# A decoder layer on one core: when GpSimd may subtract in the early tiles, and an output projection in four steps

## The reference, cut to what matters

```
x = x + self_attention(layernorm(x))           # 16 heads of 16, 4 key/value heads, projection @ Wo + bo
x = x + cross_attention(layernorm(x), context) # 77 context rows
x = x + ffn(layernorm(x))                      # shared expert + the 2 best of 8 experts, by a softmax gate
```

## Time and profile before

| | |
|---|---|
| median of 3 runs | 1723.9 us (1721.14 to 1726.04) |
| the profiled execution | 1722.33 us, its span 1720.6 us, mean granted clock 0.980 |
| PE busy | 1665.3 us (97%) |
| DVE busy | 1386.6 us (81%) |
| ACT busy | 1097.4 us (64%) |
| POOL busy | 399.6 us (23%) |
| output projection | 744.6 to 805.5 us |
| early tiles with routing | 1185.8 to 1244.1 us |

### The profile page before, as it was taken

The page is one execution under the profiler, slowest core; times in us unless marked ns, Lnnn a source line. Parts: engine busy times, 40 slices in busy tenths (PEclk is TensorE's granted clock), DMA queues, the critical chain, the costliest instruction groups (busy, mean ns, idle before and its releaser), DMA issues. The chain is left out here.

```text
span 1720.6 us, 35427 instructions
## 1 busy us (share of the span) xinstructions
PE 1665.3 (97%) x11830; PEld 1092.0 (63%) x11831; DVE 1386.6 (81%) x2603; ACT 1097.4 (64%) x2272; POOL 399.6 (23%) x462
## 2 busy tenths in 40 slices
PE   7899999999999999999999999997899999999998
PEld 3443333333333333366689999996798888888887
DVE  6699999999999999634688999985897666666664
ACT  5348888888888888842577777774325455554552
POOL 2000000000000000041042222222472554555540
PEclk9869999999999999999999999998999999999999
DMA  6612111111111111153311321114525333333335
GB/s 217 196 20 36 33 32 30 31 30 30 30 31 30 30 31 31 37 169 109 120 49 43 105 99 52 41 56 155 188 78 169 55 49 54 52 52 55 49 58 169
DMA packets 93594, 124.80 MB, mean 73 GB/s; under 512 B 19307, under 2 KB 72863, under 8 KB 92863
## 3 DMA queue, kind: packets, MB, share of 16 engines
q1 hardware_dynamic: 75696, 99.34, 20.4%
q0 software_dynamic: 13728, 18.88, 6.8%
q10 hardware_dynamic: 4047, 4.91, 0.9%
HBM read 71.25 MB, written 46.60 MB: 68 GB/s over the span
## 5 line engine op out<-in xcount | busy, mean ns | idle before, releaser
L506 DVE TENSOR_REDUCE half_max<-psA 128x1 f32<-128x512 f32 x1024 | 630.1, 683 | 6.7 <-PE psA L559 4.6
L538 ACT ACTIVATE PT<-psB 128x1024 f32<-128x1024 f32 x512 | 520.8, 1026 | 140.1 <-PE psB L569 139.7
L559 PE MATMUL psA<-KS,QS 48*128 48x512 f32 x1024 | 397.5, 470 | 8.0 <-PEq L104 2.0
L569 PE MATMUL psB<-QS,KS 50*128 50x512 f32 x1024 | 377.8, 457 | 0.1
L588 PE MATMUL psO<-PT,VG 128*32 128x256 f32 x4096 | 321.0, 392 | 0.1
L559 PEld LDWEIGHTS psA<-KS,QS 48*128 48x128 f32 x1024 | 163.3, 191 | 232.8 <-DVE half_max L506 172.9
L588 PEld LDWEIGHTS psO<-PT,VG 128*32 128x32 f32 x4096 | 84.6, 108 | 176.2 <-issue 102.8
L1405 ACT ACTIVATE x_probs<-x_scores,x_neg_max 128x77 f32<-128x77 f32 x512 | 176.3, 359 | 6.4 <-DVE x_neg_max L1308 6.3
L1880 PE MATMUL m_psY<-swd_high,m_hT 128*128 128x256 f32 x760 | 157.8, 291 | 0.4 <-DVE m_hT L2034 0.2
L569 PEld LDWEIGHTS psB<-QS,KS 50*128 50x128 f32 x1024 | 150.9, 186 | 10.7 <-ACT PT L538 9.5
L475 POOL CAST max_parts<-neg_max 128x16 fp32r<-128x16 f32 x32 | 6.3, 197 | 618.4 <-DVE neg_max L516 618.4
(11 more groups left out here) (235 smaller groups left out, 2727.2 us busy)
## 6 DMA issues: line engine op xcount, KB each, us to landing
QS<-q_parts SPq DMA_DIRECT2D x96, 128.0 KB
q_parts<-part SPq DMA_DIRECT2D x16, 512.0 KB, 4.3
OT<-OU SPq DMA_DIRECT2D x16, 512.0 KB, 3.5
mx_kept<-cx_mx SPq DMA_DIRECT2D x8, 616.0 KB, 5.4
cx_mx<-mx_kept SPq DMA_DIRECT2D x4, 1232.0 KB, 7.7
KS<-k_parts SPq DMA_DIRECT2D x32, 128.0 KB
xf_rows<-XF SPq DMA_DIRECT2D x32, 128.0 KB, 1.7
acc<-X SPq DMA_DIRECT2D x32, 128.0 KB, 1.8
```

The lines of the kernel that those rows point to most:

```text
L506: dve.tensor_reduce(half_max[:, h * (TB // 2) + t % (TB // 2), n:n + 1], psA[:, bank_of(slot, 2 * v + r), :], axis=AX.X, op=ALU.max).then_ ...
L538: act.activation(PT[:, k % 4, 2 * a:2 * a + 2, :].rearrange("p h n -> p (h n)"), psB[:, u % 2, :, :].rearrange("p a n -> p (a n)"), ACT.Ex ...
L559: pe.matmul(psA[:, bank_of(slot, m), :], QS[top:top + KQ, slot, h // 2, t * P:(t + 1) * P], KS[top:top + KQ, slot, n * HALF:(n + 1) * HALF ...
L569: mm = pe.matmul(psB[:, u % 2, r, :], KS[top:top + KM, slot, c * P:(c + 1) * P], QS[top:top + KM, slot, a, half * HALF:(half + 1) * HALF], ...
```

## The change

Two independent edits.

In the output projection the copies to OT are gone: psR's transposes read OU itself. TensorE's step n now runs psR of tile n, psU of tile n-2 and psY of tile n-3, and VectorE's addition to X moves to the same step as psY. VectorE's loop is written out.

In the early tiles VectorE raises a new semaphore `pieces_done` after each first and each second piece. Up to step 8 GpSimd waits for the first piece of step s before it subtracts tile s, and for the second before it subtracts a weight part. Weight parts are halves (128x512), one in each of the steps 1 to 8, which makes two experts instead of three; the third expert's matrices join those of VectorE (12 instead of 10, up to step 24). ScalarE's casts for the first experts begin at step 1 instead of 2, and SP no longer waits in step 3.

```
-POOL_EXPERTS = 3
+POOL_EXPERTS = 2
-POOL_FROM = 2
+POOL_FROM = 1
+POOL_HALVES = KD * POOL_SPLITS
...
             for s in range(EARLY_TILES):
+                if s < HOT_AT:
+                    pool.wait_ge(pieces_done, 2 * s + 1)
                 if low_on_pool(s):
                     token_low(s)
-                for k in splits_at(s):
-                    if k < POOL_SPLITS:
-                        weight_part_low(k)
+                if 0 <= s - POOL_FROM < POOL_HALVES:
+                    pool.wait_ge(pieces_done, 2 * s + 2)
+                    weight_half_low(s - POOL_FROM)
...
+            def weight_half_low(n):
+                k, half = divmod(n, KD)
                 x, m = SPLITS[k]
                 w, high, low = SPLIT[m]
                 pool.wait_ge(w_high, k + 1)
+                pool.tensor_tensor(low[:, x, half, :], w[:, x, half, :], high[:, x, half, :], ALU.subtract).then_inc(lows_pool, 1)
...
                 if beside:
                     first_piece(now[0])
+                    dve.sem_inc(pieces_done, 1)
...
                 if beside:
                     second_piece(now[0])
+                    dve.sem_inc(pieces_done, 1)
```

The projection, TensorE's part (VectorE's addition moves from `tile(2)` to `tile(L_OUT)`; all of `load_rows` and its waits go):

```
+        L_TURN, L_OUT = 2, 3
...
             def step(tile):
+                if t := tile(0):
+                    i, e = t
+                    if not peeled(i, 2):
+                        pe.wait_ge(norm_done, at(i, 1, -1))
+                    for g in range(NKV):
+                        mm = pe.transpose(psR[:, e, g * P:(g + 1) * P], OU[:, g, i * P:(i + 1) * P], ident[:, :])
+                    mm.then_inc(rows_done, 1)
+                if t := tile(L_TURN):
...
+                if t := tile(L_OUT):
...
-            for n in range(NT + 2):
+            for n in range(NT + L_OUT):
```

More of the change, by code:

```diff
@@ L647, in self_out_places @@
     offset = T["place"]["QS"] + 4608
-    for name, shape in (("wo_sb", [P, KD, D]), ("bo_sb", [P, D]), ("OT", [P, 2, NKV, 2 * P])):
+    for name, shape in (("wo_sb", [P, KD, D]), ("bo_sb", [P, D])):
         T[name] = nc.alloc_sbuf_tensor_at(name, shape, F32, offset=offset)
@@ L651, in self_out_places @@
     assert offset <= T["place"]["QS"] + 4 * 2 * (GH // 2) * S
-def load_rows(eng, T, n):
-    eng.dma_start(T["OT"][:, n % 2, :, :], T["OU"][:, :, 2 * n * P:(2 * n + 2) * P]).then_inc(T["so_sums_in"][n % 2], 16)
 def load_self_out(eng, T):
@@ L661, in load_self_out @@
     eng.dma_start(T["bo_sb"][:, :], T["bo"].rearrange("(a n) -> a n", a=1).to_broadcast([P, D])).then_inc(T["so_w_in"], 16)
-    for n in range(2):
-        load_rows(eng, T, n)
 def phase_self_out(nc, T):
@@ L674, in sem @@
             return ctx.enter_context(nc.semaphore(name))
-        wo, bo, OT, w_in, sums_in = (T[k] for k in ("wo_sb", "bo_sb", "OT", "so_w_in", "so_sums_in"))
+        wo, bo, OU, w_in = (T[k] for k in ("wo_sb", "bo_sb", "OU", "so_w_in"))
+        L_TURN, L_OUT = 2, 3
         recip = sb("recip", [P, 2, NH])
@@ L693, in phase_self_out @@
         block = ctx.enter_context(nc.Block())
[L695 to L701, removed]
         @block.gpsimd
@@ L714, in step @@
             def step(tile):
-                if t := tile(2):
+                if t := tile(0):
[6 more added lines that the diff above has]
+                if t := tile(L_TURN):
+                    i, e = t
+                    pe.wait_ge(norm_done, at(i, 1, 1))
+                    if not peeled(i, 2):
+                        pe.wait_ge(turned_in, at(i, 1, -1))
+                    for k in range(KD):
+                        mm = pe.transpose(psU[:, e, k * P:(k + 1) * P], ON[:, e, k * P:(k + 1) * P], ident[:, :])
+                    mm.then_inc(turned, 1)
+                if t := tile(L_OUT):
                     i, e = t
@@ L763, in step @@
                     dve.tensor_tensor(X[:, i, :], psY[:, e, 0:D], X[:, i, :], ALU.add).then_inc(x_added, 1)
-            staggered(dve, NT, (0, 1, 2), step)
+            for n in range(NT + L_OUT):
+                step(lambda lag, n=n: (n - lag, (n - lag) % 2) if 0 <= n - lag < NT else None)
         @block.scalar
@@ L1459 @@
 SPLITS = [(x, m) for x in range(NE) for m in range(2)]
-POOL_EXPERTS = 3
+POOL_EXPERTS = 2
 POOL_SPLITS = 2 * POOL_EXPERTS
-POOL_FROM = 2
+POOL_FROM = 1
+POOL_HALVES = KD * POOL_SPLITS
+assert POOL_FROM + POOL_HALVES <= HOT_AT
 def splits_at(s):
@@ L1482, in lows_on_pool @@
 def lows_on_pool(i):
-    return sum(low_on_pool(s) for s in range(i + 1)) + sum(k < POOL_SPLITS for s in range(i) for k in splits_at(s))
+    return sum(low_on_pool(s) for s in range(i + 1)) + sum(POOL_FROM <= s < POOL_FROM + POOL_HALVES for s in range(i))
 def load_turned(eng, T, n):
@@ L1619, in phase_ffn @@
         tile_hot = sem("r_tile_hot")
-        sums_done = sem("r_sums_done")
+        sums_done, pieces_done = sem("r_sums_done"), sem("r_pieces_done")
         w_in, wd_in = sem("m_w_in"), sem("m_wd_in")
@@ L1784, in token_low @@
                 pool.tensor_tensor(xT[1][:, e, :, :], turned_tile(i, e), xT[0][:, e, :, :], ALU.subtract).then_inc(lows_pool, 1)
-            def weight_part_low(k):
+            def weight_half_low(n):
+                k, half = divmod(n, KD)
                 x, m = SPLITS[k]
@@ L1789, in weight_part_low @@
                 pool.wait_ge(w_high, k + 1)
-                pool.tensor_tensor(low[:, x, :, :], w[:, x, :, :], high[:, x, :, :], ALU.subtract).then_inc(lows_pool, 1)
+                pool.tensor_tensor(low[:, x, half, :], w[:, x, half, :], high[:, x, half, :], ALU.subtract).then_inc(lows_pool, 1)
             def hot_values(q):
@@ L1802, in _ @@
             for s in range(EARLY_TILES):
+                if s < HOT_AT:
+                    pool.wait_ge(pieces_done, 2 * s + 1)
                 if low_on_pool(s):
                     token_low(s)
-                for k in splits_at(s):
-                    if k < POOL_SPLITS:
-                        weight_part_low(k)
+                if 0 <= s - POOL_FROM < POOL_HALVES:
+                    pool.wait_ge(pieces_done, 2 * s + 2)
+                    weight_half_low(s - POOL_FROM)
                 if 0 <= s - HOT_AT < NHOT:
                     hot_values(s - HOT_AT)
-            pool.wait_ge(lows_pool, POOL_LOWS + POOL_SPLITS)
+            pool.wait_ge(lows_pool, POOL_LOWS + POOL_HALVES)
             pool.wait_ge(slots_done, 6)
@@ L1843, in step @@
                     if isinstance(i, int) and i == EARLY_TILES:
-                        pe.wait_ge(lows_pool, POOL_LOWS + POOL_SPLITS)
+                        pe.wait_ge(lows_pool, POOL_LOWS + POOL_HALVES)
                         pe.wait_ge(w_low, len(SPLITS) - POOL_SPLITS)
@@ L2179, in decoder_layer @@
             T["so_w_in"] = attention.enter_context(nc.semaphore("so_w_in"))
-            T["so_sums_in"] = [attention.enter_context(nc.semaphore(f"so_sums_in_{e}")) for e in ("even", "odd")]
             with ExitStack() as stacks:
```

## The result

The changed kernel takes 1702.3 us in the median (1700.65 to 1713.24) against 1723.9 (1721.14 to 1726.04): a ratio of 0.987, 95% interval [0.983, 0.990]. The forecast was 1704.

The account below looks back on a forecast made before the run. The prediction took TensorE, with short waits on other engines, as the bound. Savings of 9.6 + 11.5 less 0.9 and 0.5 made 19.7 us: 1722.33 to 1702.6, about 1704 as median; range 1698 to 1713, 8 in 10.

Parts of the forecast that it names:

- Projection, 9.6 predicted: Output projection: 1.56 us per tile instead of 1.83, stage 51.2 us against 60.85, so 9.6 us saved.
- The rule: Output projection: a busy PE is modelled, so idle time has to be read on the weight-load queue.
- By themselves they are worth nothing: Output projection: removing 16 OT loads gains nothing alone, as TensorE waited 0.2 us for them in all; the order counts.
- The fourth step: Output projection: running psR(n), psU(n-2), psY(n-3) gives ON, and likewise ONT, over a whole step to be ready.
- Early tiles, 11.5 predicted: Early tiles with routing: GpSimd's holds on VectorE shrink, steps take 4.64 us, 38.5 instead of 50.0, so 11.5 us saved.
- 0.9 lost at the start: Start of early tiles: GpSimd's first token subtraction waits for VectorE's r_ex, delaying TensorE's first matmul by 0.9 us.
- ScalarE's earlier cast: Early tiles: first weight cast, a step earlier, waits for expert 0 but ends about when m_hT is due; cost nothing.
- 0.5 at the first routed tile: First routed tile: VectorE's last added weight subtraction starts behind m_xT and delays psG, 0.5 us lost, or 0 with slack.
- 1.83 per tile: Rival, output projection: interval stays near 1.83 us because loads and matmuls fill it; 1711.5 us, chance 0.11.
- holds that only move: Rival, early tiles: GpSimd's halves hold other two-operand VectorE instructions; 8.2 us saved, 1715.7 us, chance 0.09.
- neither half working: Rival, both stretches: another wait ends last in each; 2.3 - 1.4 us saved, about 1723 us, chance 0.04.
- The slower rival: Output projection: TensorE's clock falls in the starting transposes and stays low; 36 us lost against 10.1 gained, 1750, chance 0.04.

Follow-up runs that it names:

- c1: The changed kernel run once more, unmodified, beside the kernel before on the same chip: 1703.9 us, ratio 0.989.
- p2: Kernel before with psR reading OU in place and the 16 copies to OT gone, TensorE's old order of three steps kept: 1722.9 us, ratio 1.000.
- p3: Kernel before with the new four-step order psR(n), psU(n-2), psY(n-3), but the copies to OT kept: 1720.4 us, ratio 0.998.
- p4: Changed kernel with three steps in the projection instead of four: psR(n), psU(n-1), psY(n-2), sums read in place: 1703.7 us, ratio 0.989.
- t3: Changed kernel with GpSimd subtracting whole 128x1024 matrices in four steps instead of eight halves, waits for the pieces kept: 1706.3 us, ratio 0.991.
- t2: Changed kernel without GpSimd's waits for VectorE's pieces, halves kept: 1705.3 us, ratio 0.990.
- b1: Changed kernel with first token subtraction not waiting, expert 0's loads issued earlier, third to eighth experts' splits begun one step earlier: 1703.9 us, ratio 0.988.
- t1: Kernel before with only the early tiles' edit, projection left as it was: 1712.0 us, ratio 0.993.
- t4: Changed kernel in which GpSimd's token subtractions don't wait for the first piece, while weight halves still wait for the second: 1704.6 us, ratio 0.990.
- p1: Kernel before with only the projection's edit, early tiles left as they were: 1711.3 us, ratio 0.992.

## Why the prediction was right

The sum was 19.7 us; c1's profile, beside the one of before, has 10.9 in the projection and, from r_ones to the end of the span, 1720.6 - 1185.75 - (1698.0 - 1173.08) = 9.9. The medians differ by 21.6 in the first comparison and 20.3 in the one of c1.

- **Projection, 9.6 predicted, 10.9 measured.** Counted to the end of the last addition, as in the prediction, the stage is 49.98 us: psR(4) 3.75 behind the first psR, 27 intervals of 1.52, and 5.17 behind the last psR, where 3.8, 27 x 1.56 and 5.3 were forecast. The size that was off is the interval, 1.1 of the 1.2 us. The prediction took psY's wait of 0.27 off and held psU's to be in the mean already. By the earlier trace rows and their counterparts after, the idle time of the load queue before its three groups fell from 18.3 to 6.8 us while its busy time grew from 44.3 to 45.7, which makes 0.32 per tile. The rule held that what can be won is the idle time of the load queue, and not that of the busy-looking PE.
- **"By themselves they are worth nothing", of the copies.** True as written (p2), but the next sentence, that the order counts, left out what would be late next with the copies still there: 8.0 of the 10.9 us are lost without the reading in place (p3). The terms were right because the change does both; the reason given covers half.
- **The fourth step** was taken for what gives ON and ONT room. p4 shows that the order within the step does it.
- **Early tiles, 11.5 predicted, 10.9 and 11.4 measured.** 4.64 per step holds from tile 2 on. The step with the counting matmuls took 6.12 and 6.04, 1.4 to 1.5 more, where 0.82 and 0.5 were put for them, and its wait for r_both was 0.31. So this came as worked out, and so did VectorE's busy time without holds (28.7 forecast, 28.9 measured). That a VectorE instruction with an operand in PSUM isn't held by GpSimd is what t3 shows most plainly: m_y and m_hT run at their usual 0.42 and 0.69 beside a whole subtraction, and r_value is held for its rest. The Trainium skill ("SBUF — State Buffer", section Who interferes with whom) says that VectorE instructions with two SBUF inputs contend with a GpSimd instruction that reads SBUF, that copies, casts and tensor-scalar operations can contend with it in their faster modes, and that in such a mode whoever issues first has the shared pair of ports for its whole instruction. The held rows here agree, the TENSOR_SCALAR of 128x8 with 1.22 us in t2 among them; which mode an instruction ran in, no row shows.
- **0.9 lost at the start** was too much. psG does come 0.68 later behind r_ones (3.09 against 2.41), but m_psH of tile 0 comes on average 8.87 behind r_ones in the five profiles where the first token subtraction waits, and 8.62 in the eight where it doesn't: 0.25, inside a spread of 0.7 among the five. Of tile 0's twelve matmuls the first run at the lower clock (0.63 each) and the last at the higher (0.40): the last one to four where the first token subtraction waits, none to two where it doesn't. So a later start had fewer of them at the lower clock, which gives part of the delay back.
- **ScalarE's earlier cast, "nothing"**: it waits 2 to 3.2 us for WU in every kernel with the edit but b1 (0.51), and m_hT stands behind it. The step from tile 0 to tile 1 is none the longer in c1 and p4 (4.71, 4.70), but takes 4.97 to 5.39 in the changed kernel's first profile, t1 and t4. The price of nothing should have been a range from 0 to 0.7.
- **0.5 at the first routed tile**: 0.65, gone in b1.
- **The rivals.** 1.83 per tile, holds that only move, and neither half working are all excluded by the intervals. The slower rival, a clock that falls in the transposes, did not come: the granted clock is 1.00 over the first 5 us of the stage, whose first 2.8 us are transposes alone, and over all of it. The Trainium skill ("TensorE: Matmul & The Clock Gate", Part 4: PE-mode transpose) says that the higher clock doesn't engage for transposes. Here it stayed, in a stretch that began with the clock already high (1.00 from 740 on, in the attention); no run here begins transposes at the lower level, so whether they could raise it isn't shown.

## What to carry to other kernels

When an interval shrinks, price every transfer and every wait that hid behind it against the new interval, also the ones that showed no wait: here removing a copy without the reorder gave 0.1 us, the reorder without removing the copy 2.9, both 10.9. Where GpSimd and VectorE both read SBUF, place GpSimd's work beside VectorE's PSUM instructions or cut it into pieces near VectorE's spare time per step (pieces of 1.3 us, about a microsecond spare); here the two waits alone got 5.0 and the halves alone 3.9 of the 6.1 to 6.6 us that both got. And in a software-pipelined loop try another order within the step before adding a step.

## What the runs showed of the hardware

- The attention's first stretch varies from run to run with TensorE's clock: from 80 to 160 us PE is busy for over 99% in both profiles shown above, yet the granted clock is 0.50 and 0.69 in one and 0.58 and 1.00 in the other, and the work behind starts 12.2 us later. That is more than half of what the whole change saves, and falls on kernels with and without it: p2's clock was 0.92 from 120 to 160, and the kernel before, run beside p1, took 1730.5 us at a mean clock of 0.974 and 1720.3 at 0.982. Why the clock stays down there isn't shown.
- A hold on VectorE lasts for the rest of GpSimd's instruction, whatever the held one's size: held instructions took 0.84 to 1.22 us beside halves in t2 and 1.06 to 2.35 beside whole matrices, on 128x8 as on 128x256. In the rows above they end 0.04 to 0.28 us after GpSimd's.
